# VectorE scales k in place of GpSimd; SyncE issues layer 3's chunk 1 copies ahead of x2's first half

## What is computed

```python
xn = (xe - bn_mean) * (bn_gamma * rsqrt(bn_var + BN_EPS)) + bn_beta
q, k, v = split(xn @ w_qkv + b_qkv, 3, axis=2)
q = q - mean(q, axis=2);  k = k - mean(k, axis=2)
q2, k2 = q * q, k * k
q2 = l2n(q2 / (sum(q2, axis=2) + 1e-07), axis=2)
k2 = l2n(k2 / (sum(k2, axis=2) + 1e-07), axis=1)     # "scale k": the division by the sum
kv = einsum('bnc,bnd->bcd', k2, v)                   # "attention sums"
```

## Time and profile before

| | us |
|---|---|
| median of 3 runs | 1057.41 (1055.5 to 1058.46) |
| profiled execution | 1057.32 |
| its span, first to last instruction | 1055.5 |
| TensorE busy | 979.3, 93% |
| VectorE busy | 864.2, 82% |
| ScalarE busy | 473.1, 45% |
| GpSimd busy | 94.3, 9% |
| mean granted TensorE clock | 0.978 of full speed |

### The profile page before, as it was taken

One profiled execution on the slowest core, in us unless ns is written; L12 is line 12 of the kernel. 1 busy time (PEld: TensorE's weight loads), 2 busy tenths in 40 slices (PEclk: granted clock), 3 DMA queues, 4 the chain that ended last, 5 costly groups with the idle time before them and its releaser, 6 DMA issues.

```text
span 1055.5 us, 14771 instructions
## 1 busy us (share of the span) xinstructions
PE 979.3 (93%) x4598; PEld 625.8 (59%) x4598; DVE 864.2 (82%) x1231; ACT 473.1 (45%) x813; POOL 94.3 (9%) x120
## 2 busy tenths in 40 slices
PE   5689869999999999999999999999999999987986
PEld 4456656666665675666665576666665676654624
DVE  6762568999599968999599968999599977998980
ACT  2311435355633645355533646355533646334522
POOL 0210003001300003001300003001200013000000
PEclk9799979999999999999999999999999999999998
DMA  5242815176534665175534666175534666145315
GB/s 73 51 124 48 146 31 134 38 124 136 119 82 84 114 133 144 36 122 126 129 82 79 110 134 151 36 122 120 129 88 74 110 135 154 36 84 118 71 31 102
DMA packets 129520, 104.48 MB, mean 99 GB/s; under 512 B 97903, under 2 KB 98772, under 8 KB 129492
## 3 DMA queue, kind: packets, MB, share of 16 engines
q1 hardware_dynamic: 129492, 104.14, 48.0%
HBM read 10.82 MB, written 6.29 MB: 16 GB/s over the span
## 4 chain that ended last, share of the span: by engine, by line
PE 55%; DVE 20%; issue 10%; SPq 8%; DMA 4%; ACT 2%; DVEq 0%; ACTq 0%
PE bank L1307 26%; DVE dwa L713 9%; PE bank L1287 5%; PE bank L1339 4%; PE bank L1313 4%; SPq L1015 3%; PE bank L1354 3%; DMA y_parts<-a_parts 3%; PE bank L1355 3%; DVE dwa L729 2%; PE bank L1277 2%; PE bank L1323 2%; DVE dwb L729 2%; SPq L1055 2%; PE bank L1342 1%
## 5 line engine op out<-in xcount | busy, mean ns | idle before, releaser
L713 DVE SCALAR_TENSOR_TENSOR dwa<-h1a,dyn,dwa 128x1024 f32<-128x1024 f32 x224 | 280.9, 1277 | 1.0
L1307 PE MATMUL bank<-y_parts,w_l 128*96 128x512 f32 x576 | 151.2, 407 | 0.0
L1307 PE MATMUL bank<-y_parts,w_h 128*96 128x512 f32 x576 | 147.6, 400 | 0.0
L713 DVE SCALAR_TENSOR_TENSOR dwb<-h1b,dyn,dwb 128x1024 f32<-128x1024 f32 x112 | 142.9, 1276 | 0.5
L1339 PE MATMUL bank<-a_parts,wt_h 128*112 128x512 f32 x384 | 117.4, 414 | 14.6 <-DMA y_parts<-a_parts 12.5
L1307 PEld LDWEIGHTS bank<-y_parts,w_l 128*96 128x96 f32 x576 | 91.6, 163 | 61.1 <-issue 21.4
L1307 PEld LDWEIGHTS bank<-y_parts,w_h 128*96 128x96 f32 x576 | 92.9, 161 | 44.3
L1339 PEld LDWEIGHTS bank<-a_parts,wt_h 128*112 128x112 f32 x384 | 64.1, 175 | 50.1 <-issue 28.4
L1164 POOL TENSOR_TENSOR y_low<-y,y_parts 96x512 fp32r<-96x512 f32 x56 | 67.3, 1202 | 224.6 <-DVE y L767 224.6
L1157 POOL TENSOR_TENSOR tok<-tok,u 128x1536 f32<-128x1536 f32 x8 | 22.4, 2804 | 566.5 <-DVE u L628 566.5
L1287 PE MATMUL bank<-xq,w_cur 97*96 97x512 f32 x128 | 68.0, 613 | 3.7 <-DVE y L767 3.7
(11 more groups left out here) (268 smaller groups left out, 1655.6 us busy)
## 6 DMA issues: line engine op xcount, KB each, us to landing
y_parts<-y_parts SPq DMA_DIRECT2D x32, 396.0 KB, 3.5
y_parts<-a_parts SPq DMA_DIRECT2D x64, 198.0 KB, 3.0
y_parts<-a_parts SPq DMA_DIRECT2D x64, 197.6 KB, 3.5
tok<-in_x_dram SPq DMA_DIRECT2D x48, 192.0 KB, 4.9
y_parts<-y_low SPq DMA_DIRECT2D x64, 132.0 KB, 3.3
a_parts<-a_parts SPq DMA_DIRECT2D x128, 66.0 KB, 2.5
x_even<-y_parts SPq DMA_DIRECT2D x32, 198.0 KB, 3.7
x_odd<-y_parts SPq DMA_DIRECT2D x32, 198.0 KB, 4.0
```

What stands on the lines that cost most here:

```text
L713: nc.vector.scalar_tensor_tensor(out=dst, in0=tap_input(n, t), scalar=weight, in1=dst, op0=ALU.mult, op1=ALU.add).then_inc(tap_step, 1)
L1307: nc.tensor.matmul(bank[0:C2, :], wgt[:, t, :], y1_parts[:, part, rows, cols], start=part + t == 0, stop=False)
```

## The change

`scale_k` moves from GpSimd's stream to VectorE's, right behind `factors_of_k`. In the loop and in iteration 0, `squares_of_q` moves behind layer 3's last low part and x2's last two low parts, next to `factors_of_q`. On SyncE the copies of layer 3's chunk 1 move ahead of x2's first half, in the loop alone. The last iteration is not changed, other than by what GpSimd does.

```diff
+            def scale_k(image):
+
+                dve.wait_ge(u_ready, 2 * image + 1)
+                k = tokens(K_AT)
+                nc.vector.tensor_tensor(k, k, columns(u[:, :, :], 2 * RUN, [[1, 2 * RUN], [0, C]]), ALU.mult).then_inc(k_scaled, 1)
...
                 if back is not None:
                     l3_low_part(back, 2)
                 factors_of_k()
-                squares_of_q()
+                scale_k(attn)
                 mean_out(f)
-                factors_of_q()
                 if back is not None:
                     l3_low_part(back, 3)
                 x2_low_part(f, 2)
                 x2_low_part(f, 3)
+                squares_of_q()
+                factors_of_q()
...
             factors_of_k()
+            scale_k(0)
             squares_of_q()
...
                 if back is not None:
-                    beside_l3(sp, back, f + 1, (0,))
+                    beside_l3(sp, back, f + 1, (0, 1))
                 copy_x2(sp, f, 0)
                 if back is not None:
-                    beside_l3(sp, back, f + 1, range(1, PCHUNKS))
+                    beside_l3(sp, back, f + 1, (2, 3))
                 copy_x2(sp, f, 1)
...
-            def scale_k(image):
-                pool.wait_ge(squared, 16 * image + 16)
-                pool.wait_ge(u_ready, 2 * image + 1)
-                k = tokens(K_AT)
-                nc.gpsimd.tensor_tensor(k, k, columns(u[:, :, :], 2 * RUN, [[1, 2 * RUN], [0, C]]), ALU.mult).then_inc(k_scaled, 1)
...
-            scale_k(0)
             split_y1(0)
             with pool.Fori(1, IMAGES) as image:
-                scale_k(image)
                 split_y1(image)
```

## The result

| | before | after |
|---|---|---|
| median | 1057.93 (1055.5 to 1060.5, 4 runs) | 1082.88 (1082.73 to 1083.94, 4 runs) |
| ratio | | 1.024, 95% interval 1.0222 to 1.0258 |
| span of the profiled execution | 1055.5 | 1081.0 |
| TensorE waiting for layer 3's copies | 12.5 us, 14 times | 28.7 us, 10 times |
| mean granted TensorE clock | 0.978 | 0.967 |

The change makes the kernel 25 us slower, and the forecast was 1082.5.

A forecast was written before the change was run, and what follows sets the result against it. TensorE bounds the loop and hangs on SyncE's DMA stream at layer 3's chunks 1 and 2. From 1057.32 us, + 15.0 (queue) + 7.8 (clock) + 2.4 (prologue and iteration 0) = 1082.5, range 1072.5 to 1088.

The forecast's parts named there:

- The queue: SyncE in the loop: chunk 2's copies go later and delay TensorE 2.5 us in each of six iterations, 15.0 us.
- Rival (c): Layer 3's copies in the loop land sooner without x2's DMAs ahead, so not slower: 1054.1 us; chance 0.04.
- (d): Loop unchanged, as chunk 2 waits for ScalarE; delayed copies would still arrive at 382.8, so a form of the forecast.
- The clock: TensorE behind the joined 4.0 us gap in the loop: clock falls, 1.3 us in each of six iterations, 7.8 us.
- Rival (a): Loop: queue delay as forecast, but the clock holds or falls in one or two iterations; 1074.7 to 1077.5 us; chance 0.26.
- (b): Loop: the low clock spreads and an iteration loses another 1.0 us, 1088.5 us; chance 0.09.
- k on VectorE in the loop: VectorE's added multiplication of 1.76 us makes route 1.2 us late, covered by idle time: cost nothing, gain nothing.
- Prologue and iteration 0: Ahead of the loop: VectorE's longer chain +0.7 us, late squares of q in iteration 0 +1.7 us; together 2.4 us.
- VectorE's chain: Prologue: VectorE's work up to q's scaling takes 1.76 us more, nearly 1.2 comes back; +0.7 us, bounds 0 and 1.76.
- the wait for L852: Iteration 0: TensorE's 5.3 us wait for VectorE grows to about 7 us, as the squares of q come late.
- the loop's 22.8 us: Six loop iterations: 15.0 us for chunk 2's later copies and 7.8 us for the clock behind the longer gap.

The follow-up runs named there:

- Experiment 4: Kernel before, with x2's first half issued behind layer 3's chunk 3 copies in the loop, ahead of its second half: 1080.58 us, ratio 1.0219.
- experiment 5: Kernel before, with three of x2's four first-half DMAs left ahead of chunk 1's copies and the fourth behind chunk 3's: 1054.04 us against 1058.09, ratio 0.9959.
- experiment 3: Changed kernel, with 12 added matmuls filling TensorE's gap ahead of layer 3's chunk 2 in each loop iteration: 1076.66 us, ratio to before 1.0166.
- experiment 2: Changed kernel with SyncE's old order, so only VectorE's part is changed (k's scaling, late squares of q): 1060.85 us against 1057.62, ratio 1.0027.
- experiment 7: Changed kernel with SyncE's old order and the squares of q in their old place, so only GpSimd's work moves: 1059.54 us against 1058.09, ratio 1.0011.
- experiments 1: Kernel before with only SyncE's order changed; GpSimd scales k as before: 1080.79 us against 1057.62, ratio 1.021.
- experiment 6: Kernel before, with x2's first half issued by ScalarE in the loop, SyncE issuing layer 3's copies in one go: 1079.67 us, ratio 1.0204; second run 1079.61.

## Why the prediction was right

**The queue (15.0 us forecast).** From x2's low part 1 to chunk 2's matmuls it was 8.44 + 6.99 = 15.43 us and is 10.75 + 7.12 = 17.87 (388.45 - 381.33 for the second term): 2.44 in iteration 2. Over iterations 1 to 5 the distance from the attention sums to chunk 2 grew from 8.54 to 10.94 us on the mean, by 2.40, so 14.4 to 14.6 in all; with the gap filled, the iterations gave 2.0 to 2.4. I had 2.5. The parts were off in opposite directions: SyncE reacted 0.10 us after low part 2 and not 0.25, the ten DMAs took 7.95 and not 8.19 us, but the copies behind x2's did not land sooner (7.12 and not 6.74). Taking all of it as not made good later was right: VectorE's loop order and every later stage moved along. Experiment 4 shows why the argument holds, since another order with the same idle time costs the same. Rival (c) needed 4.4 us from chunk 2's first issue to its matmuls, and it is 7.12; (d) falls with the readings under experiment 5.

**The clock (7.8 us).** It fell behind all six gaps of 3.74 to 4.13 us. 3.68 - 2.44 = 1.24 an iteration, 7.4 in all, against 1.3 and 7.8; filling the gap gave about 6 us back with five falls of six gone, and its undisturbed iterations allow up to 1.7 for a fall. What a fall costs in work is 1.4 to 1.5 us (experiment 3); the net is less, since the changed kernel's iterations have less waiting behind chunk 2 (in the kernel before, iterations 1, 3 and 4 wait 0.2 to 0.4 us more there, for chunk 3's copies or the input). The Trainium skill's rule of a wait for a DMA that lets the clock fall at each tile (TensorE: Matmul & The Clock Gate, HAM oscillation) held here, in six of six, at 7.4 us net where I had put the term's upper end at 9 us. Rival (a), which rested on one gap of 3.21 us without a fall, did not come about. Nor did (b): an iteration lost 3.68 us, no more than queue and fall explain.

**k on VectorE in the loop (nothing).** Right by experiment 2: 119.31 us. `route` comes at 379.78, 6.5 us behind the end of low part 2, where it was 5.4; L826's successor L832 takes 0.35 us instead of 1.19, as reckoned. The multiplication takes 1.76 us, the duration of L656, and not the 1.4 us that the ratio in the GPSIMD Engine Reference (Engine selection) of the Trainium skill would give.

**Prologue and iteration 0 (2.4 us).** The sum was right (2.5 after, 2.1 in experiment 2), its terms were not, so its fit is in part luck. In the prologue I counted VectorE's chain, + 0.7, which is what it shows. But the earlier k lets TensorE finish the attention sums earlier and wait longer for the chain:

```profile
40.48 0.51 PE L1256 MATMUL bank<-twin,gs 112*97 112x48 f32 x2 [2.79 <-DVE gs L670]
...
42.03 1.09 PE L1277 MATMUL bank<-ident,tok 128*96 128x128 f32 x4
...
47.84 0.60 PE L1277 MATMUL bank<-ident,tok 128*96 128x128 f32 x4
```

Before, that gap was 0.69 us and the last of these lines stood at 46.55, so the prologue cost 1.3 us: behind the longer gap the clock was at 1.2 GHz from about 40.6 to 47.4 us, where it had been from 42.4 to 45.8. So 0.5 us of the 1.3 are VectorE's chain (0.7 us, less 0.2 by which it starts earlier; `gs` is read at 39.88 and not 39.37), and 0.8 us are the clock. I had written that the earlier end of TensorE's wait gains nothing; in this trace it goes with a loss. That the earlier k is the cause of the longer stretch at 1.2 GHz is argued and not shown: experiment 4, whose prologue is that of the kernel before, has one from about 40.3 to 47.2 us behind a gap of 1.57 us. Still, the attention sums of iteration 0 start at 134.11 to 134.83 us in the five profiles with k on GpSimd, and at 135.39 to 136.46 in the four with k on VectorE.

Iteration 0 then cost 2.5 - 1.3 = 1.2 us and not 1.7. The squares of q do come late, by 1.7 us, but not where I looked for it: the wait for L852 stayed at 5.3 us and didn't grow to 7. VectorE's `sums_apart` stands behind the squares, too, and the wait for it grew instead:

```profile
140.88 0.37 PE L1256 MATMUL bank<-twin,gs 112*97 112x48 f32 x2 [2.29 <-DVE gs L670]
```

It was 0.56 us, and it is 0.57 in experiment 7, with the squares in their old place. I had left out who is queued behind the moved instruction first.

**What was left out.** 0.9 us in iteration 7, which the change doesn't touch: the clock fell three times there in the changed kernel and in experiments 1 and 2, two times before. The length of a gap does not tell it here: the same wait of 3.21 us ahead of L1407 was followed by a fall in the changed kernel and not in the kernel before. The total agrees more closely than its terms: the loop's 22.8 us were 22.1, and these 0.9 us make up for the difference.

## What to carry to other kernels

When DMAs in one queue wait for different producers, look at the time that the queue idles, not at which transfer is wanted first: moving a transfer whose data is late ahead of one whose data is there delays everything behind both. Put into the idle time what fits, here three DMAs of four, and the rest behind. And price a gap on TensorE with what follows it: here two short gaps joined into one of 3.7 to 4.1 us, which cost an iteration about 1.2 us beyond the added idle time.

## What the runs showed of the hardware

Issuing from a second engine bought nothing here: with four DMAs issued by ScalarE in 3.5 us, SyncE's six took 7.6 us instead of 4.0, and all ten 7.6 us instead of 7.95 (experiment 6). The Trainium skill (DMA: Bandwidth & Descriptors, Issuing engines are not separate DMA queues) says that issuing on several engines at once saves the sequencers' time to initiate; in this trace little of that time was saved, and the measurement decides for this kernel.

Whether the clock falls behind a gap is not told by the gap's length. Gaps of 2.72 to 3.13 us (experiment 4) were followed by 1.2 GHz in six of six iterations, and those of 3.74 to 4.13 us of the changed kernel, too. One of 3.10 us in the changed kernel's iteration 7 (ahead of the matmul at 970.43) was not, and the clock was at 1.2 GHz from about 999.7 us, soon behind one of 1.04 us (ahead of the matmul at 998.95).

A wait on TensorE that ends earlier need not win time: in the prologue k came 1.3 us earlier, the gap behind the attention sums went from 0.69 to 2.79 us, and the stretch at 1.2 GHz behind it from 3.4 to 6.8 us.
